# Parameter loads on ScalarE's queue, seven images' first statistics on ScalarE, and VectorE's set-up between the first loads

## What is computed

```python
x = x + _L0_conv_ref(_gn(x), L0_conv_accumulators)
x = x + _L1_conv_ref(_gn(x), ..., L1_conv_adj_w, L1_conv_affine_w, L1_conv_affine_b, L1_conv_ln_g, L1_conv_ln_b)
```

## Time and profile before

| | |
|---|---|
| median of 3 runs | 1118.68 us (1114.17 to 1120.12) |
| profiled execution | 1114.09 us, span 1112.4 us |
| PE busy | 1036.8 us (93%) |
| ACT busy | 912.6 us (82%) |
| DVE busy | 803.6 us (72%) |
| DMA from HBM | 136.45 MB |

### The profile page before, as it was taken

The page is one execution under the profiler, slowest core; times in us unless marked ns, Lnnn a source line. Parts: engine busy times, 40 slices in busy tenths (PEclk is TensorE's granted clock), DMA queues, the critical chain, the costliest instruction groups (busy, mean ns, idle before and its releaser), DMA issues.

```text
span 1112.4 us, 19839 instructions
## 1 busy us (share of the span) xinstructions
PE 1036.8 (93%) x7160; PEld 785.9 (71%) x7160; DVE 803.6 (72%) x1389; ACT 912.6 (82%) x1706; POOL 534.2 (48%) x266
## 2 busy tenths in 40 slices
PE   1299999968999999999999999999999999999996
PEld 0055555546887777777777777777777778887774
DVE  7723555578777777777777777777777777777767
ACT  1799999448888888888888888888888888888885
POOL 0044454513355555555555555555555555555533
PEclk9999999979999999999999999999999999999998
DMA  8989999730122222222232233222222222222212
GB/s 355 404 338 403 408 419 412 297 152 20 58 77 77 77 76 77 76 77 77 100 110 97 96 106 104 96 77 85 81 99 80 76 77 77 77 78 77 77 58 96
DMA packets 33120, 158.59 MB, mean 143 GB/s; under 512 B 4232, under 2 KB 4860, under 8 KB 22780
## 3 DMA queue, kind: packets, MB, share of 16 engines
q1 hardware_dynamic: 33020, 157.29, 37.3%
HBM read 136.45 MB, written 20.83 MB: 141 GB/s over the span
## 4 chain that ended last, share of the span: by engine, by line
PE 83%; DMA 7%; DVE 4%; POOL 2%; ACT 2%; issue 2%; SPq 1%; POOLq 0%; ACTq 0%; DVEq 0%
PE PS L1224 21%; PE PS L1225 21%; PE PS L1226 21%; PE PS L1242 5%; PE PS L1199 5%; PE PS L1189 4%; DMA Wt<-acc 4%; PE PS L1210 2%; DMA X<-x 2%; PE PS L1236 2%; PE PS L1230 2%; DVE st L759 1%; SPq L296 1%; DMA NU<-factor_rows 1%; POOL X L436 0%
## 5 line engine op out<-in xcount | busy, mean ns | idle before, releaser
L941 DVE TENSOR_TENSOR Pl<-PS,Ph 128x512 fp32r<-128x512 f32 x512 | 347.7, 690 | 184.1 <-ACT PS L609 179.2
L609 ACT ACTIVATE PS<-PS 128x512 f32<-128x512 f32 x512 | 305.4, 610 | 9.5 <-PE PS L1226 9.3
L608 ACT ACTIVATE Ph<-PS 128x512 fp32r<-128x512 f32 x384 | 234.4, 610 | 95.0 <-PE PS L1226 92.0
L1224 PE MATMUL PS<-Ph,hh 128*128 128x512 f32 x512 | 206.5, 403 | 1.2 <-DVE Pl L941 1.2
L1224 PE MATMUL PS<-uTh,nTh 128*128 128x512 f32 x512 | 199.8, 390 | 0.9 <-DVE uTl L915 0.9
L1225 PE MATMUL PS<-Pl,hh 128*128 128x512 f32 x512 | 200.1, 391 | 0.0
L1226 PE MATMUL PS<-uTh,nTl 128*128 128x512 f32 x512 | 199.6, 390 | 0.0
L1225 PE MATMUL PS<-uTl,nTh 128*128 128x512 f32 x512 | 199.6, 390 | 0.0
L1226 PE MATMUL PS<-Ph,hl 128*128 128x512 f32 x512 | 199.6, 390 | 0.0
L422 POOL TENSOR_TENSOR hl<-X,hh 128x1024 fp32r<-128x1024 f32 (+1 forms) x33 | 77.2, 2339 | 195.8 <-ACT hh L593 169.8
L405 POOL TENSOR_TENSOR LL<-LL 128x512 f32<-128x512 f32 x64 | 82.5, 1289 | 135.5 <-ACT LL L497 135.5
(11 more groups left out here) (142 smaller groups left out, 1600.3 us busy)
## 6 DMA issues: line engine op xcount, KB each, us to landing
Wt<-acc SPq DMA_DIRECT2D x64, 1024.0 KB, 7.4
out<-X SPq DMA_DIRECT2D x38, 512.0 KB, 2.7
X<-x SPq DMA_DIRECT2D x16, 1024.0 KB, 19.7
SQ<-norm_rows SPq DMA_DIRECT2D x31, 512.0 KB, 3.6
X<-factor_rows SPq DMA_DIRECT2D x31, 512.0 KB, 4.1
NU<-factor_rows SPq DMA_DIRECT2D x31, 512.0 KB, 5.0
X<-out SPq DMA_DIRECT2D x7, 512.0 KB, 5.8
out<-X SPq DMA_DIRECT2D x2, 256.0 KB, 2.1
```

Of the source, the lines that this page charges most:

```text
L608: act.activation(Ph[:, g % RING, :], sl, ACT.Exp, scale=SHARP)
L609: act.activation(sl, sl, ACT.Exp, scale=SHARP).then_inc(weights_ready, 1)
L941: dve.tensor_tensor(Pl[:, r, :], SL[r], Ph[:, r, :].bitcast(F32), ALU.subtract)\
L1224: pe.matmul(out_, lh, rh, start=start, stop=False)
```

## The change

The five parameter loads are issued on ScalarE's queue ahead of its table load, so SyncE's queue begins with x. ScalarE makes the first statistics of seven images (6, 9, 12, 17, 20, 25, 27) instead of four, three of them ahead of the exponentials of batch 0, two between the exponentials of batches 0 and 1, and two behind those of batch 1. The batches' sums now wait for two, five and seven of them. VectorE's set-up is cut into three parts that stand behind the pieces of loads 0, 1 and 2.

```diff
--- before.py
+++ after.py
@@ -39,8 +39,8 @@
 
 BATCHES = ((0, 0, 12), (0, 12, 22), (0, 22, 32), (1, 0, 4), (1, 4, 32))
 
-BY_ACT = (13, 17, 23, 25)
-ACT_UPTO = (0, 2, 4)
+BY_ACT = (6, 9, 12, 17, 20, 25, 27)
+ACT_UPTO = (2, 5, 7)
 AT_ONCE = 5
 
 
@@ -288,10 +288,6 @@
 
         @block.sync
         def _(sp):
-            sp.dma_start(adj_sb[:, :], adj_w).then_inc(params_loaded, 16)
-            sp.dma_start(aff_sb[:, :], aff_w).then_inc(params_loaded, 16)
-            for t, v in ((bcol, aff_b), (lbc, ln_b), (gcol, ln_g)):
-                sp.dma_start(t[:, :], v.rearrange("(c o) -> c o", o=1)).then_inc(params_loaded, 16)
             for i in range(LOADS):
                 sp.dma_start(X[:, i * IPL:(i + 1) * IPL, :],
                              x[:, i * IPL:(i + 1) * IPL, :]).then_inc(image_loaded[i], 16)
@@ -473,6 +469,10 @@
 
         @block.scalar
         def _(act):
+            act.dma_start(adj_sb[:, :], adj_w).then_inc(params_loaded, 16)
+            act.dma_start(aff_sb[:, :], aff_w).then_inc(params_loaded, 16)
+            for t, v in ((bcol, aff_b), (lbc, ln_b), (gcol, ln_g)):
+                act.dma_start(t[:, :], v.rearrange("(c o) -> c o", o=1)).then_inc(params_loaded, 16)
             act.preload_act_table_set("natural_log_exp_and_others")
             act.wait_ge(setup_products, 3)
             act.activation(squares[:, :], SETUP[:, 2 * C:3 * C], ACT.Square, accum_out=col[:, :]).then_inc(gram_squared, 1)
@@ -521,18 +521,19 @@
 
 
             act.wait_ge(flag_ready, 1)
-            for i in range(3):
-                if i == 0:
-                    statistics(0)
-                if i == 1:
-                    statistics(2)
-                    statistics(3)
-                roots(i)
-                if i == 0:
-                    statistics(1)
-                if i < 2:
-                    act.wait_ge(stat_steps, NS * (i + 1))
-                    exps(0, range(*BATCHES[i][1:]))
+            for j in (0, 1, 2):
+                statistics(j)
+            roots(0)
+            act.wait_ge(stat_steps, NS)
+            exps(0, range(*BATCHES[0][1:]))
+            for j in (3, 4):
+                statistics(j)
+            roots(1)
+            act.wait_ge(stat_steps, 2 * NS)
+            exps(0, range(*BATCHES[1][1:]))
+            for j in (5, 6):
+                statistics(j)
+            roots(2)
 
             lo, hi = BATCHES[2][1:]
             act.wait_ge(stat_steps, NS * 3)
@@ -741,18 +742,23 @@
 
         @block.vector
         def _(dve):
-            dve.wait_ge(params_loaded, 16 * 5)
-            dve.wait_ge(consts_made, NCONST)
-            dve.tensor_scalar(bB[:, :], ident[:, :], 0.0, bcol[:, :], ALU.mult, ALU.add).then_inc(setup_steps, 1)
-            dve.tensor_copy(Whi[:, :], adj_sb[:, :]).then_inc(setup_steps, 1)
-            dve.wait_ge(setup_steps, 2)
-            dve.tensor_tensor(Wlo[:, :], adj_sb[:, :], Whi[:, :].bitcast(F32), ALU.subtract).then_inc(setup_steps, 1)
-            dve.wait_ge(setup_products, 2)
-            dve.tensor_copy(Ac[:, :], SETUP[:, 0:C]).then_inc(setup_steps, 1)
-            dve.tensor_scalar(b1[:, :], SETUP[:, C:2 * C], KAPPA, None, ALU.add).then_inc(setup_steps, 1)
-            dve.wait_ge(bound_summed, 1)
-            dve.tensor_scalar(flag[0:1, 0:1], SETUP[0:1, 3 * C:3 * C + 1], SHARP**4, LIMIT**4, ALU.mult, ALU.is_le)\
-                .then_inc(flag_ready, 1)
+            def setup_operands():
+                dve.wait_ge(params_loaded, 16 * 5)
+                dve.wait_ge(consts_made, NCONST)
+                dve.tensor_scalar(bB[:, :], ident[:, :], 0.0, bcol[:, :], ALU.mult, ALU.add).then_inc(setup_steps, 1)
+                dve.tensor_copy(Whi[:, :], adj_sb[:, :]).then_inc(setup_steps, 1)
+                dve.wait_ge(setup_steps, 2)
+                dve.tensor_tensor(Wlo[:, :], adj_sb[:, :], Whi[:, :].bitcast(F32), ALU.subtract).then_inc(setup_steps, 1)
+
+            def setup_values():
+                dve.wait_ge(setup_products, 2)
+                dve.tensor_copy(Ac[:, :], SETUP[:, 0:C]).then_inc(setup_steps, 1)
+                dve.tensor_scalar(b1[:, :], SETUP[:, C:2 * C], KAPPA, None, ALU.add).then_inc(setup_steps, 1)
+
+            def setup_flag():
+                dve.wait_ge(bound_summed, 1)
+                dve.tensor_scalar(flag[0:1, 0:1], SETUP[0:1, 3 * C:3 * C + 1], SHARP**4, LIMIT**4, ALU.mult, ALU.is_le)\
+                    .then_inc(flag_ready, 1)
 
             def piece(turn, m, b):
                 w = NPOS // PIECES[turn]
@@ -776,7 +782,7 @@
             def batch_sums(i):
                 _, lo, hi = BATCHES[i]
                 dve.wait_ge(stat_pieces, i + 1)
-                if i in (1, 2):
+                if i < 3:
 
                     dve.wait_ge(act_steps, 5 * ACT_UPTO[i])
                 if i:
@@ -834,6 +840,8 @@
                     if b not in BY_ACT:
                         for m in range(PIECES[0]):
                             done = piece(0, m, b)
+                if i < 3:
+                    (setup_operands, setup_values, setup_flag)[i]()
                 if (i + 1) * IPL in [hi for _, _, hi in BATCHES[0:3]]:
                     done.then_inc(stat_pieces, 1)
```

## The result

| | before | after |
|---|---|---|
| median | 1115.26 us (5 runs, 1114.17 to 1120.12) | 1129.47 us (5 runs, 1128.44 to 1130.50) |
| profiled span | 1112.4 us | 1126.9 us |
| first product of layer 0 | 56.04 us | 68.80 us |
| from there to the end of the span | 1056.4 us | 1058.1 us |
| DVE busy | 803.6 us | 799.7 us |

The ratio is 1.0117, 95% interval [1.0096, 1.0139], which is 10.7 to 15.5 us slower. The first product is late by 68.80 - 56.04 = 12.76 us, so the loss lies in the opening. The likeliest forecast had +7.1. By the medians the change costs 1129.47 - 1115.26 = 14.2 us; the single executions of the kernel before lie up to 6 us apart, so the first product tells the size better.

A forecast was written before the change was run, and what follows sets the result against it. The prediction took the opening up to the first product as the bound. Its steps put batch 2's sums at 56.2 against 49.05, +7.1 us; 1118.7 + 7.1 = 1125.8 us, range 1119.5 to 1129.5.

The forecast's parts named there:

- What bounds the kernel: Opening up to the first product at 56.04 us: x's stream, what is left over after it, a 6.99 us tail.
- one for one to the end: Behind the opening: the weights' stream starts from the first product, so its shift passes to the end in full.
- part is won back: Rival, weights' stream: a later first product finds awaited chunks landed, +7.1 shrinks to +4.7, 1123.4 us; chance 0.10.
- ScalarE's order: Batches 1 and 2: sums wait for images behind exponentials, VectorE idles some 6 and 5 us; batch 2's sums at 56.2.
- So I take no wait: Set-up: parameters land between 4.8 and 12.7 us, load 0's pieces end at 9.4, so VectorE waits 0 us.
- parameters late: Rival, set-up: parameter packets take turns with x's; landing at 12.7 us gives +10, 1128.8 us; chance 0.08.
- scales 0 at 28.3: Batch 0: its scales done on VectorE at 28.3 us, against 29.33 before, a gain of 1.0 us.
- x's lead: Start of x's stream: five issues gone from SyncE's queue bring x 1.7 us earlier, with ends 0 and 2.34.
- parameters cost the DMA engines 0.62 us: x's stream: parameters beside x still take 0.62 us of DMA time, subtracted from 2.34 to give 1.7.
- the even spacing: x's loads: arrivals drawn back from loads 12 and 13 at 2.49 us per load.
- ScalarE's statistics from 15.7 at no cost: ScalarE's first images: start at 15.7 us, two done at 21.8, in time for batch 0's sums at 22.0.
- The flag: End of VectorE's set-up, which ScalarE's statistics wait for: 15.7 us instead of 8.6.

The follow-up runs named there:

- c2: c1 with the two columns that only attention needs issued behind all of x and awaited ahead of attention: first product 55.55 us, ratio 1.0002.
- b1: The kernel before with the changed kernel's seven ScalarE images, each batch's images ahead of the exponentials that stood before them: first product 55.37 us, ratio 0.9990.
- b3: The changed kernel with set-up awaiting three of five parameter loads, the two columns awaited only ahead of attention: first product 63.66 us, ratio 1.0075.
- c1: The kernel before with the parameters behind x's first load on SyncE's queue and set-up behind loads 0, 1 and 2: first product 55.59 us, ratio 0.9993.
- a4: The kernel before with only the changed kernel's seven ScalarE images, their order and the batches' waits: first product 64.03 us, ratio 1.0060.
- b2: The changed kernel with the five parameter loads issued on SyncE's queue between x's first and second load: first product 63.80 us, ratio 1.0065.
- a1: The changed kernel with the five parameter loads on SyncE's queue ahead of x again: first product 63.88 us, ratio 1.0062.
- c3: The changed kernel with b2's place of the parameters and b1's order of images: first product 55.21 us, ratio 0.9989.
- a2: The changed kernel with SyncE's queue waiting for all five parameters before x's first load: first product 65.51 us, ratio 1.0084.

## Why the prediction was right or wrong

**What bounds the kernel, and one for one to the end: right.** In the twelve kernels the part behind the first product shows no trend with it, and each ratio's interval holds the first product's shift. The rival "part is won back" did not come: from the first product on PE waited 2.9 us for weights, against 2.4 before. In the opening one thing was put wrongly: batch 2's sums hang on load 13 and VectorE's work behind it (c2), not on the last load.

**ScalarE's order: right in place and size.** From batch 0's scales to batch 1's the forecast had 46.1 - 28.3 = 17.8 us, the trace 51.76 - 34.14 = 17.6. From there to batch 2's sums it had 10.1, the trace 61.81 - 51.76 = 10.05. b1 confirms the cause: the place of the images, not their number.

**The parameters: wrong.** "So I take no wait" is the step that failed. My latest landing, five loads one after another at 2.0 us each, gave 12.7; they landed at 15.7. I had looked at their share of the DMA engines, 0.62 us, and argued from it against the rival. Share isn't the measure: the number of packets is, since each column more lands 2.5 us later and b3, which waits for two fewer, gains 5.1 us. That the size of the other queue's packets sets how long a turn takes is my reading of the counts; no run changed that size. The rival "parameters late" was the true case, with 8 chances in 100 from me, and its +10 was still too small. By my own steps, scales 0 at 28.3 became 34.1, 5.8 us later, and that is the whole difference between +7.1 and +12.8 (5.7).

The Trainium skill ("DMA: Bandwidth & Descriptors", Queues, rings and completion order) says that each DMA engine goes round the queue rows with work, a packet at a time. The counts of 93 to 94 and 99 to 100 agree, if a packet of the profile is one of the page's; the 57 to 155 from 5 to 6 us is no such turn for turn. I had weighed another sentence of that page and not this one.

**x's lead: right in sign, too large.** I took 1.7 us of 2.34; c1 shows 0.45 at loads 12 and 13. With the parameters beside x it is no better: b3 has load 5 at 20.20, against 20.54 in a4. The term "parameters cost the DMA engines 0.62 us" was mis-sized: in line they cost x's stream 1.9 (c1) to 2.1 us (b2). In the changed kernel itself the term did not count, since from 15.69 us on VectorE never waits for x. An opposite error stood beside it: in a4 and a1 load 5 arrives 0.65 and 0.8 us sooner than the even spacing gave. So a4 and a1 came at 64.0 and 63.9 where I expected 64.8 and 64.9.

**ScalarE's statistics from 15.7 at no cost: wrong by the same cause.** The flag came at 21.5, batch 0's sums waited 1.46 us for ScalarE's second image.

**The range** held the median by a hair (1129.47 against 1129.5), and that was luck. Its upper end stood for a shift of at most 1129.5 - 1118.7 = 10.8 us, and the shift was 12.8; it fitted only because the 1118.7 on which I had built is 3.4 us above the median of before with more runs.

## What to carry to other kernels

Ask of a transfer that moves to another queue not how many bytes it has but how many packets, and what stands on the queue beside it: 720 small packets beside a stream of 8 KB packets landed 12.8 us after the last issue instead of 2.1, and any engine waiting for them waits too. When work goes to another engine, follow that engine's order from each of its waits to the next. Here the same seven images cost 8 us behind the exponentials and nothing ahead of them.

## What the runs showed of the hardware that was not expected

Packets of 4 bytes on one queue and of 8 KB on another passed in equal numbers (99 to 100 in 2 us), so that each column of 128 such packets took 2.5 us. In line on one queue behind a load of x the same five loads land in 3.7 to 4.6 us (b2, c1, c3), but 1.75 us of the DMA engines' time are lost. With nothing beside them, loads issued on ScalarE's queue land as soon as on SyncE's (2.1 us in a2 and in the kernel before).

The first 64 product matmuls took 3.64 us in the kernel before and 1.98 us in the changed one. The others fell on either side (3.64 or 3.65 in a1, a4, b1 and c1, 1.98 in the rest), and the granted clock reads 1.00 in both. The cause was not sought; the part behind the first product shows no gain from it.
